# Maxima over partitions by transposes and small matmuls, and FFN weights prepared earlier, in a fused attention and FFN kernel

## The reference

```
x = x + layernorm(attention(layernorm(x)))
x = x + layernorm(ffn(layernorm(x)))
```

```
base = x @ W_base + b_base
h = relu(x @ Wd1[e] + bd1[e]);  recon = h @ Wd2[e] + bd2[e]
idx = argmin over e of mean((recon - x)**2)
out = base + relu(x @ Wa_down[idx] + ba_down[idx]) @ Wa_up[idx] + ba_up[idx]
```

## Time and profile before

| what | us |
|---|---|
| median of 3 runs | 2296.5 (2293.96 to 2301.31) |
| the profiled execution | 2299.66 |
| its span, first to last instruction | 2297.9 |
| busy PE / DVE / ACT / POOL | 2019.7 / 1479.1 / 861.0 / 703.4 |

### The profile page before, as it was taken

How to read it: one execution, slowest core, us unless ns; L and a number is a source line. 1 busy time by engine, 2 the same in 40 slices (tenths; PEclk the granted TensorE clock), 3 DMA queues, 4 the chain that set the end, 5 groups by cost and what they waited for, 6 DMA issues and landing times.

```text
span 2297.9 us, 58734 instructions
## 1 busy us (share of the span) xinstructions
PE 2019.7 (88%) x24985; PEld 1307.0 (57%) x24985; DVE 1479.1 (64%) x3330; ACT 861.0 (37%) x1492; POOL 703.4 (31%) x918
## 2 busy tenths in 40 slices
PE   1787999989899998989999898999989899998945
PEld 0464755647475564747556474755647475564724
DVE  2657676676767667676766767676676767767532
ACT  2333434343343434334343434434343343434221
POOL 4026232331513233152323315232331523223051
PEclk9879999999999999999999999999999999999978
DMA  5223222151422215142231514122151422214020
GB/s 124 54 47 81 41 78 63 25 125 30 117 42 77 64 20 130 30 116 43 77 64 24 126 30 118 41 78 63 23 126 30 116 43 77 64 31 100 12 55 19
DMA packets 232971, 150.70 MB, mean 66 GB/s; under 512 B 153035, under 2 KB 203732, under 8 KB 232693
## 3 DMA queue, kind: packets, MB, share of 16 engines
q1 hardware_dynamic: 232710, 146.95, 27.2%
HBM read 36.98 MB, written 16.78 MB: 23 GB/s over the span
## 4 chain that ended last, share of the span: by engine, by line
PE 61%; DVE 17%; SPq 7%; issue 5%; POOL 4%; ACT 3%; DMA 2%; DVEq 1%; POOLq 0%; ACTq 0%
PE NS L942 11%; PE ringF L1150 9%; SPq L424 7%; PE ringF L1135 6%; PE KV L1023 5%; PE ringA L1109 5%; PE ringA L843 4%; PE ringF L1185 3%; PE ringA L1009 3%; PE ringA L985 3%; DVE mx L1485 3%; DVE stage L1575 3%; PE ringF L843 2%; PE ringF L1187 2%; ACT E L686 2%
## 5 line engine op out<-in xcount | busy, mean ns | idle before, releaser
L1150 PE MATMUL ringF<-x,H 128*128 128x256 f16 x1536 | 237.9, 273 | 0.0
L1499 DVE TENSOR_REDUCE mx<-ringA 128x8 f32<-128x512 f32 x256 | 175.6, 686 | 90.1 <-PE ringA L985 89.5
L678 ACT ACTIVATE E<-ringA,score_scale 128x512 f32<-128x512 f32 x256 | 175.6, 686 | 117.4 <-PE ringA L1009 117.2
L843 PE MATMUL ringA<-xT,wqkv 128*128 128x512 f16 x768 | 187.1, 395 | 26.5 <-ACT QS L696 11.7
L1150 PE MATMUL ringF<-H 128*128 128x128 f16 x1024 | 204.4, 220 | 1.4 <-DVE H L1586 1.4
L1552 DVE SCALAR_TENSOR_TENSOR X<-X,NS 128x320 f32<-128x320 f32 x160 | 78.0, 488 | 180.9 <-PE NS L942 175.8
L1485 DVE TENSOR_REDUCE mx<-ringA 128x1 f32<-128x512 f32 x256 | 160.3, 683 | 50.8 <-PE ringA L976 50.2
L1135 PE MATMUL ringF<-wd,x2T 128*128 128x512 f16 x768 | 188.1, 385 | 5.0 <-DVE H L1586 3.4
L513 POOL TENSOR_SCALAR vtmp<-mv,eps_ffn 128x8 f32<-128x8 f32 x16 | 5.1, 318 | 610.4 <-DVE mv L1328 610.4
L686 ACT ACTIVATE E<-ringA,score_scale 128x512 f32<-128x512 f32 x256 | 158.8, 685 | 78.4 <-PE ringA L1040 78.4
L513 POOL TENSOR_SCALAR vtmp<-mv,eps_ln 128x8 f32<-128x8 f32 x32 | 10.0, 312 | 544.3 <-DVE mv L1328 536.6
(11 more groups left out here) (251 smaller groups left out, 4309.3 us busy)
## 6 DMA issues: line engine op xcount, KB each, us to landing
KS<-stage SPq DMA_DIRECT2D x384, 64.0 KB, 2.0
QS<-stage SPq DMA_DIRECT2D x384, 64.0 KB, 2.0
xin<-in_L_attn_x_dram SPq DMA_DIRECT2D x16, 1024.0 KB, 11.0
xres<-in_L_attn_x_dram SPq DMA_DIRECT2D x16, 1024.0 KB, 8.1
out_dram<-yout SPq DMA_DIRECT2D x16, 1024.0 KB, 5.5
QS<-LB SPq DMA_DIRECT2D x16, 512.0 KB, 4.4
E<-in_L_attn_w_qkv_dram SPq DMA_DIRECT2D x1, 768.0 KB, 7.1
H<-in_L_ffn_Wd_dram SPq DMA_DIRECT2D x2, 256.0 KB
```

The lines of the kernel that those rows point to most:

```text
L678: A(E[:, k % ESLOTS, :], ps[:, :], ACT.Exp, scale=score_scale[:, 0:1]).then_inc(freed["s3"].sem, 1)
L843: ins = MM(dst, left(a, k), right(c, k), start=n == 0, stop=n == 3 * KC - 1)
L1150: ins = MM(dst, H[:, a, t, own], src, start=first and i == 0, stop=last and i >= 3, skip_group_check=True)
L1499: V_.reduce_max(mx1[:, t, 8 * h:8 * h + 8], take(b, "m1", k)[:, :].rearrange("p (a m) -> p a m", a=8), AX.X)\
```

## The change

Both reductions over partitions leave POOL. DVE's `amax` is transposed on PE (4 rows of 128), DVE takes the maximum of each row (`mxr`) and writes it 128 times along the row (`mxb`), and PE multiplies that with a 4 x 4 identity, which gives the four maxima on all 128 partitions in PSUM, columns 80 to 84 of `ringF[1]`. `scales` reads them there. POOL's remaining constants go behind `norm1(0)`. The FFN's maxima are taken at k = 2 (`ffn_rows`) and its scales at k = 3 of batch 0's inversion. `ffn_reduction` goes from the end of DVE's batch 0 to ACT, behind the inversion. ACT's copy of the transposed Wd2 goes ahead of its high half of batch 1.

```
--- POOL
             assert made[0] == POOL_ATTN
+            def later_constants():
+                step(pool.memset(eye_ns[:, :], 0.0))
...
-            pool.wait_ge(s_set.sem, 2)
-            step(pool.partition_all_reduce(amax_all[:, :], amax[:, 0:4], P, bass.bass_isa.ReduceOp.max))
             def ffn_weights():
-                pool.wait_ge(s_set.sem, DVE_FFN_MAX)
-                step(pool.partition_all_reduce(amax_all[:, :], amax[:, 0:4], P, bass.bass_isa.ReduceOp.max))
                 pool.wait_ge(s_set.sem, DVE_FFN_SCALES)
...
             norm1(0)
+            later_constants()
--- ACT
+            def ffn_reduction():
+                act.wait_ge(s_set.sem, DVE_FFN_SCALES)
+                act.wait_ge(s_setp.sem, POOL_CONSTS)
+                for e in range(2):
+                    rows = slice(e * HID, (e + 1) * HID)
+                    for q in range(EP):
+                        ins = A(rcol[rows, q:q + 1], ringF[1][rows, q * NE + 2 * q + e:...], ACT.Copy)
+                ins.then_inc(s_red.sem, 1)
+                for e in range(2):
...
+                    A(R2[rows, :, e * HID:(e + 1) * HID], blocks, ACT.Identity, scale=hid_sc[rows, 0:1])
+                    A(R2[rows, :, P + C + e * HID:P + C + (e + 1) * HID], blocks, ACT.Identity, scale=hid_sc[rows, 3:4])
...
+                for q in range(EP):
+                    ins = A(R2[:, q, P:P + C], f_w2[:, q, :], ACT.Identity, scale=hid_sc[:, 1:2], bias=rcol[:, q:q + 1])
...
+                if first(b):
+                    ffn_reduction()
                 for k in range(ESLOTS, 2 * ESLOTS):
                     exp1(b, k)
--- PE
+                    pe.wait_ge(s_set.sem, DVE_FFN_MAX)
+                    TR(ringF[1][0:4, P:2 * P], amax[:, 0:4], identf[:, :])
...
+                elif part == 3:
+                    pe.wait_ge(s_set.sem, DVE_FFN_ROWS)
+                    MM(ringF[1][:, 80:84], mxb, identf[0:4, 0:4], start=True, stop=True).then_inc(s_setpe.sem, 1)
--- DVE
+            def maximum_rows(ps):
+                step(V_.reduce_max(mxr, ps, AX.X))
+                step(V_.tensor_copy(mxb, mxr.to_broadcast([4, P])))
...
-            dve.wait_ge(s_setp.sem, POOL_QKV)
+            dve.wait_ge(s_qkvpe.sem, 1)
+            maximum_rows(ringF[0][0:4, 0:P])
+            dve.wait_ge(s_qkvpe.sem, 2)
             scales(slice(0, 1))
...
             amx(amax[:, 3:4], f_dn, AX.XY)
+            dve.wait_ge(s_setp.sem, POOL_CONSTS)
...
+                        if first(b) and k == 2:
+                            ffn_rows()
+                        if first(b) and k == 3:
+                            ffn_scales()
...
-                if first(b):
-                    ffn_scales()
...
                 statistics(b, 1, ao, freed["pr"], 2)
-                if first(b):
-                    ffn_reduction()
```

More of the change, by code:

```diff
@@ L316, in sandwich_kernel @@
         POOL_EARLY = 16
+        POOL_ATTN = 21
         POOL_CONSTS = 34
[L318 to L325, removed]
+        POOL_DONE = POOL_CONSTS + 14
+        DVE_QKV_MAX = 2
+        DVE_QKV_ROWS = 4
+        DVE_QKV = 12
+        DVE_FFN_SUMS = 14
+        DVE_FFN_MAX = 15
+        DVE_FFN_ROWS = 17
+        DVE_FFN_SCALES = 22
         def affine(pool, t, op, fill, base, pattern, cm):
@@ L468, in _ @@
             assert made[0] == POOL_EARLY
-            for t in (KlB, QlB, Yblk):
-                step(pool.memset(t[:, :, :], 0.0))
+            step(pool.memset(KlB[:, :, :], 0.0))
+            step(pool.memset(QlB[:, :, :], 0.0))
             kf = KlB[0:4 * PAIRS, :, :].rearrange("p a (j m) -> p a j m", j=2)
@@ L473, in _ @@
             step(affine(pool, kf, ALU.not_equal, FOLD, -2, [[-4, PAIRS], [-1, 2], [0, M]], 1))
[L474 to L480, removed]
@@ L490, in _ @@
-            assert made[0] == POOL_QKV
+            step(pool.memset(Yblk[:, :, :], 0.0))
+            assert made[0] == POOL_ATTN
+            def later_constants():
+                step(pool.memset(eye_ns[:, :], 0.0))
+                step(affine(pool, eye_ns[:, :], ALU.not_equal, 3.75, 0, [[-1, M]], 1))
+                step(affine(pool, eye_ns[:, :], ALU.not_equal, 3.75, -M, [[-1, M]], 1))
+                step(pool.memset(sel32[:, :], 0.0))
+                step(pool.memset(sel32[0:M, 0:D], 1.0))
+                step(pool.memset(sel32[M:P, D:HD2], 1.0))
+                step(pool.memset(half_mask[:, :], 1.0))
+                step(affine(pool, half_mask[:, :], ALU.is_ge, 0.0, 0, [[-64, 2]], 1))
+                step(affine(pool, half_mask[:, :], ALU.is_ge, 0.0, 63, [[64, 2]], -1))
+                step(pool.memset(hid[64:65, :], 1.0))
+                step(pool.memset(R2[:, :, :], 0.0))
+                for t, v in ((onesm, 1.0), (neg1, -1.0)):
+                    step(pool.memset(t, v))
+                assert made[0] == POOL_CONSTS, made[0]
@@ L755, in body @@
                         adapter(b - 1)
+                    if first(b) and k == 0:
+                        act.wait_ge(s_setpe.sem, 1)
+                        for c in range(KC):
+                            A(f_w2T[:, c, :, :], ringF[c][:, :].rearrange("p (q n) -> p q n", q=EP), ACT.Copy).then_inc(s_w2t.sem, 1)
                     if 1 <= k < 4:
@@ L763, in body @@
                         halves1(b + 1, (k,))
[L764 to L767, removed]
                 if ffn:
@@ L1336, in split @@
                 step(V_.tensor_tensor(lo, src, hi, ALU.subtract))
+            def maximum_rows(ps):
+                step(V_.reduce_max(mxr, ps, AX.X))
+                step(V_.tensor_copy(mxb, mxr.to_broadcast([4, P])))
             def scales(cols):
-                step(V_.tensor_scalar(scale_w[:, cols], amax_all[:, cols], TINY, None, ALU.max))
+                step(V_.tensor_scalar(scale_w[:, cols], ringF[1][:, 80 + cols.start:80 + cols.stop], TINY, None, ALU.max))
                 step(V_.tensor_scalar(scale_w[:, cols].bitcast(U32), scale_w[:, cols].bitcast(U32), 0x7F800000, None, ALU.bitwise_and))
@@ L1383, in ffn_scales @@
                 V_.tensor_scalar(hid_sc[:, 1:2], scale_w[:, 1:2], -2.0, None, ALU.mult)
-                V_.tensor_scalar(hid_sc[:, 2:3], scale_w[:, 1:2], 2.0, None, ALU.mult)
+                V_.tensor_scalar(hid_sc[:, 2:3], scale_w[:, 1:2], 2.0 / (C * SHIFT), None, ALU.mult)
                 step(V_.tensor_tensor(eps_ffn[:, :], inv_w[:, 2:3], inv_w[:, 2:3], ALU.mult))
+                V_.tensor_scalar(hid_sc[:, 3:4], hid_sc[:, 0:1], 2.0, None, ALU.mult)
                 step(V_.tensor_scalar(eps_ffn[:, :], eps_ffn[:, :], EPS, None, ALU.mult))
                 assert made[0] == DVE_FFN_SCALES
[L1389 to L1405, removed]
             def take(b, kind, k):
@@ L1604, in gram @@
                     dve.wait_ge(freed["gr"].sem, freed["gr"].at(b, q))
+                if first(b) and q == 0:
+                    dve.wait_ge(s_red.sem, 3)
                 V_.tensor_tensor_reduce(out=take(b, "gr", q)[:, 0:GR], in0=bank("gr", q)[:, 0:GR], in1=R2[:, q, :], scale=1.0, scalar=0.0,
```

40 lines of the change are left out of this document (26 added, 14 removed).

## The result

The changed kernel takes 2275.5 us (2272.4 to 2281.1, 4 runs) beside 2296.1 for the kernel before (2294.0 to 2301.3). The ratio is 0.9919, 95% interval 0.9899 to 0.9938, so 14 to 23 us are gained, 20.6 by the medians. The forecast was 2273, the range 2267 to 2282. The profiled execution took 2281.05 with a span of 2279.3, 18.6 less than before, where the sum said 23.6. The granted clock is 0.964 in both.

The account below looks back on a forecast made before the run. Batches 1 to 15 were taken as bound by PE and its partners, setup and batch 0 by chains of waits. -16.8 + 1.0 - 7.8 = -23.6 gave 2276.1 from the profiled execution, 2273 from the median; range 2267 to 2282.

Parts of the forecast that it names:

- the sum: Whole kernel: start -16.8, inversion +1.0, end of batch 0 -7.8, together -23.6; ends -25.4 and -18.4.
- The start, -16.8: Up to PE's first QKV matmul: from 48.44 to 31.6, POOL's constants the last gate; ends 14.5 and 17.3.
- The small step between: POOL's norm1(0) beside DVE's QKV scaling and splitting: loses 0.5 to DVE, between nothing and about 1.76.
- POOL pays anyway: Rival at the start: the 7.63 pause is the cost of POOL's first arithmetic instruction; 7.3, 2280, chance 0.07.
- PE colder at the start: First QKV matmuls: 0.5 from a PE that starts colder after a longer pause, counted in the start's lower end.
- The inversion, +1.0: Batch 0's inversion: instructions put in on PE and DVE cost 1.0 in sum; ends +0.2 and +3.2.
- The end of batch 0, -7.8: Batch 1's start: without ffn_reduction DVE meets it like batch 2, 7.1 plus faster copies; ends 7.1 and 8.3.
- the run of copies: Batch 1's 24 copies: faster by 17.30 - 16.17 = 1.1, of which some may be chance.
- Batch 1 is held by another: Rival at batch 1's start: POOL's residual or the stage copies keep it where it was; 7.8 more, 2281, chance 0.04.
- the slower rival: PE's clock in batches 1 to 15: granted clock 0.02 less in each costs 40 more, 2313; chance 0.03.

Follow-up runs that it names:

- the split kept away: Changed kernel with DVE's constants wait behind pooled(0), FFN maxima first and the QKV weights split only after POOL's second xin; 2272.8 us, ratio 0.9903.
- the program with a late reduction: Changed kernel plus one partition_all_reduce over a constant behind POOL's constants, result unused; 2275.1 us, ratio 0.9912.
- the two repeats: The changed kernel itself timed again, without edits, beside other runs; 2277.6 us, ratio 0.9915, and 2277.7 us, ratio 0.9913.
- the FFN part alone: Changed kernel with POOL's start as before, its reduction and constants ahead of norm1(0), and everything on the FFN as changed; 2290.3 us, ratio 0.9968.
- the start alone: Changed kernel with the FFN's maxima by POOL's reduction, and scales and ffn_reduction (on DVE) at their old places; 2283.0 us, ratio 0.9937.

## Why the prediction held, step by step

**The start, -16.8.** Measured -16.0 at the first matmul. vtmp at 10.11 (10.2 said), PE's first matmul at 32.42 (31 to 33), last gate POOL's constants. The small step between was too low: I took 0.5 for what POOL loses to DVE and it was 1.9, (2.86 - 2.17) + (3.31 - 2.12), just past the upper end of 1.8; the kernel with the split kept away undoes exactly this. The sum of that upper end was itself off: 17.3 less 1.8 and 0.5 is 15.0, not 14.5, and the smallest gain of the whole 18.9, not 18.4. The reason given for the low value, that ACT's gaps would hold DVE's instructions, failed: DVE's three long ones run without a gap over 4.1 us, POOL's gap is 1.27. The Trainium skill, SBUF — State Buffer, "Who interferes with whom", has the two engines block each other for a whole instruction, where DVE's has two SBUF inputs or runs in a two-port mode; the trace agrees, with the first group 1.9 longer and the second at its old length once the split has ended at 18.79. The rival "POOL pays anyway" is excluded: the changed program's first arithmetic on POOL has no pause, and the program with a late reduction has one behind it, though vtmp had run before at 10.1.

**PE colder at the start.** The 24 first matmuls took 8.29 here, 7.14 before, but 7.08 and 7.13 in the same program's other two traces. So it is no steady price of the change.

**The inversion, +1.0.** What the changed kernel is ahead of the one before was 16.6 on PE ahead of the added instructions, 16.3 behind them and 16.7 at batch 1's first matmul. So the added instructions cost about 0.3 at most and nothing stays; batch 0 took 134.5 where I had said 1 more than 135.2. The mistake was to add durations: nearly all of them fit beside PE's score matmuls and ACT. ACT's 4.8 for ffn_reduction were hidden, as said.

**The end of batch 0, -7.8.** 11.33 became 4.20, the 7.1 that stood as the lower end; the run of copies gave 0.4, 17.30 to 16.92, where I had taken 0.7. What the prediction missed is that this gain had two owners. I named DVE alone, and gave POOL's earlier weights no value. POOL's weights caused 4.1 of DVE's 7.1 and, with DVE's share gone, held the next batch by 5.8 in the kernel that starts them late. "Batch 1 is held by another" was thus a true rival for a program that moves only ffn_reduction; the change escapes it by moving the scales to k = 3.

**The sum.** Read from the traces, 16.0 at the first matmul, 0.7 in the length of batch 0, 7.1 at its end and 0.3 in batch 1 make the 24.1 at batch 2's first copy; the forecast was 23.6. Three terms were off: the start and the end of batch 0 by 0.8 and 0.7 too good, the inversion by 1.7 too dear. That they nearly cancel is luck, and the 0.7 in the length of batch 0 lies within its scatter.

The medians gained less: 20.6, and 19.6 and 19.4 in the two repeats, whose traces are 26.3 and 26.4 ahead at batch 2's first copy. So 3.5 to 7 us of that are not found in the whole time. The kernel before has a single trace, of a run 3.6 above its median; it may have stood late at batch 2, or batches 2 to 15 may give something back. The runs don't decide this.

**The clock.** No sign of the slower rival: 0.964 before and after. But which stretches of batch 0 ran at half the clock goes with its length, 134.5, 132.2 and 132.2 in three traces of one program. In all three of them a stretch at half the clock lies behind PE's wait for DVE's sums (3.36 of idle time in the first, 2.74 in the others), and with that wait filled both traces show 1.00 there. The three traces that came to the pause at full clock (1.32 for both steps ahead) and had nothing in it all fell behind it (3.42 for the second group): two of the changed kernel and the FFN part alone. The two with the matmuls in it did not. So where PE comes at full clock, the pause causes the fall. It is not the whole rule: six traces, the first pair among them, were at half the clock two steps ahead of the pause, rose within the last step (1.57 to 1.78) and fell again behind it, and two, the start alone and the split kept away, were still at half in that step (2.15, 2.22) and came back to 1.85 in the second group, with the same pause. Why the earlier stretches fall is open.

## What to carry to other kernels

Read setup from milestones that lie just behind it, not from the whole time, in which 3.5 us of scatter per trace hide a step of 1; and take more than one trace of the kernel before. When a late instruction is taken away from one engine, look for what another engine does in the same time: here it both slowed the late one and stood next in line. The reduction on POOL cost two pauses, one ahead and one behind; either take it out, or see in the queue rows where the pause behind begins. Right behind the reduction, idle time hides it; behind a wait, POOL's next work must have 7 us to spare.

## What the runs showed that was not expected

- The pause behind POOL's reduction (7.63, 7.37) is worked off while POOL waits in one place and not in another: with 50 us between, vtmp was still 6.5 late, while the FFN weights of the kernel before started 0.2 behind their release. The row MODIFY_POOL_CONFIG came behind the wait in the first case and ahead of it in the second. The Trainium skill, GPSIMD Engine Reference, "Instruction dispatch", gives about 6 us for the first call of a freshly loaded kernel. The pauses ahead of a reduction, 5.49 to 7.25, are near that. The way back took 7.1 to 7.3 from the row to vtmp.
- Beside DVE's split two POOL selects of 128x2 rose from 0.44 to 1.25, and two of 128x64 from 0.62 to 1.90: small instructions on POOL wait too.
- Four DVE instructions took 5.37 beside one POOL instruction of 5.44, and 1.47 with none beside.
- Fourteen matmuls without use made the next two groups of PE 2.2 shorter (3.80 against 5.96 beside it): the granted clock stayed at 1.00 there, 2.4 GHz, where it had fallen to 0.59 in the mean.
